# The second sum of four groups added by TensorE instead of VectorE in the last stage

## Time and profile before

| | us |
|---|---|
| median of 3 runs | 734.59 |
| profiled execution, own time | 735.17 |
| its span, first to last instruction | 733.4 |
| TensorE busy in the span | 626.0 (85%) |
| VectorE busy | 516.5 (70%) |
| ScalarE busy | 459.2 (63%) |
| POOL busy | 395.2 (54%) |

### The profile page before, as it was taken

How to read it: one execution, slowest core, us unless ns; L and a number is a source line. 1 busy time by engine, 2 the same in 40 slices (tenths; PEclk the granted TensorE clock), 3 DMA queues, 4 the chain that set the end, 5 groups by cost and what they waited for, 6 DMA issues and landing times.

```text
span 733.4 us, 13293 instructions
## 1 busy us (share of the span) xinstructions
PE 626.0 (85%) x3690; PEld 400.4 (55%) x3690; DVE 516.5 (70%) x1472; ACT 459.2 (63%) x929; POOL 395.2 (54%) x298
## 2 busy tenths in 40 slices
PE   6988979797999848799989999999999999984640
PEld 2454636373655546466656666666666666653420
DVE  3726596968878897877877777777777777650794
ACT  3788887647575643576656776766767767661044
POOL 0004212346777676667788776666666656576022
PEclk9999999679989956999999999999999999996555
DMA  7979999773232335456678977777776766755998
GB/s 243 419 308 150 219 266 300 184 198 118 88 120 89 118 118 154 130 103 115 118 133 174 186 154 117 109 116 115 109 115 103 116 111 104 107 65 59 317 226 145
DMA packets 110695, 114.34 MB, mean 156 GB/s; under 512 B 31426, under 2 KB 100306, under 8 KB 108962
## 3 DMA queue, kind: packets, MB, share of 16 engines
q0 software_dynamic: 34784, 49.70, 40.0%
q1 hardware_dynamic: 75842, 63.79, 29.0%
HBM read 54.94 MB, written 58.51 MB: 155 GB/s over the span
## 4 chain that ended last, share of the span: by engine, by line
PE 63%; DVE 22%; ACT 5%; issue 4%; DMA 4%; POOL 1%; DVEq 0%; SPq 0%; ACTq 0%; POOLq 0%
PE PS L544 9%; PE PS L695 8%; PE PS L697 8%; PE PS L696 8%; PE PS L723 4%; PE PS L709 4%; PE PS L724 4%; PE PS L725 4%; PE PS L684 4%; PE PS L579 3%; DMA sums<-arena 3%; DVE small L1161 2%; PE PS L571 2%; PE PS L601 2%; DVE W L1321 1%
## 5 line engine op out<-in xcount | busy, mean ns | idle before, releaser
L1078 POOL DMA_INDIRECT sums<-arena x143 | 222.6, 1556 | 103.7 <-DMA sums<-arena 55.2
L1046 POOL DMA_INDIRECT routed<-arena,small x104 | 119.3, 1148 | 71.5 <-DMA routed<-arena,small 58.7
L1468 DVE TENSOR_SCALAR arena<-PS,small 128x256 f32<-128x256 f32 x143 | 77.7, 544 | 83.1 <-ACT arena L979 82.9
L544 PE MATMUL PS<-arena 128*128 128x512 f32 x256 | 130.8, 648 | 4.1 <-ACT arena L784 2.2
L979 ACT ACTIVATE arena<-PS,small 128x256 f32<-128x256 f32 x143 | 67.8, 474 | 100.2 <-PE PS L697 100.2
L784 ACT ACTIVATE arena<-PS 128x512 f16<-128x512 f16 (+1 forms) x179 | 103.9, 590 | 32.6 <-PE PS L589 11.0
L695 PE MATMUL PS<-W,arena 128*128 x286 | 109.3, 382 | 0.0
L696 PE MATMUL PS<-W,arena 128*128 x286 | 109.2, 382 | 0.0
L697 PE MATMUL PS<-W,arena 128*128 x286 | 108.9, 381 | 0.0
L723 PE MATMUL PS<-W,arena 128*128 x286 | 78.6, 275 | 6.9 <-DVE arena L1442 5.7
L724 PE MATMUL PS<-W,arena 128*128 x286 | 78.7, 275 | 0.0
(11 more groups left out here) (183 smaller groups left out, 1019.0 us busy)
## 6 DMA issues: line engine op xcount, KB each, us to landing
arena<-routed SPq DMA_DIRECT2D x143, 128.0 KB, 2.5
W<-w_gu SPq DMA_DIRECT2D x8, 1024.0 KB, 23.9
W<-neg_mem POOLq DMA_DIRECT2D x16, 512.0 KB, 9.5
sums<-zero SPq DMA_DIRECT2D x2, 4096.0 KB, 35.6
W<-sums SPq DMA_DIRECT2D x16, 512.0 KB, 8.8
X<-x SPq DMA_DIRECT2D x8, 512.0 KB, 6.2
W<-w_dn SPq DMA_DIRECT2D x4, 1024.0 KB, 11.4
out<-X SPq DMA_DIRECT2D x7, 512.0 KB, 3.2
```

Source lines behind the costliest of these rows:

```text
L544: last = mm(PS[:, 2 + c % 2, :], WcT[:, k, c * P:(c + 1) * P], xT[:, k, :], start=(k == 0), stop=(k == KT - 1))
L1046: pool.indirect_dma_start(routed, bass.IndirectOffsetOnAxis(ap=idx, axis=0), rows[b][:, jk // TOPK, :], None).then_inc(rows_sent[lane], 16)
L1078: pool.indirect_dma_start(sums[j % SUMS], bass.IndirectOffsetOnAxis(ap=dst[j % MU], axis=0), yb[u], None, compute_op=ALU.add).then_inc(y_s ...
L1468: L.send(v.tensor_scalar(up[j % 2], acc[:, FF:2 * FF], gu_hi, gu_lo, ALU.min, ALU.max))
```

## The change

For groups 1, 3, 5 and 7 the second sum no longer goes through VectorE. `biases(g)` leaves the bias open in PSUM and adds to it, for each sub-row u, the product of `identY` (the identity times `y_inv`) and `z2[g]`, an f32 product of 128 rows and 256 columns; before the first such product TensorE waits for the load of `z2[g]`. `total(g)` then has one operation for these groups. `identY` is made by VectorE in the second stage, at tile 64. TensorE now waits until all eight groups' weights are copied, computes group 0's bias, multiplies constants 150 times into bank 7, and goes on with the biases of groups 1 to 7.

```diff
--- before.py
+++ after.py
@@ -59,6 +59,8 @@
 MAGIC = float(0x5F1FFFF9)
 ROOT_A, ROOT_B = 0.375 * 0.703952253, 0.375 * 0.703952253 * 2.38924456
 SUMS = 2
+HOLD = 150
+BY_PE = (1, 3, 5, 7)
 BATCHES = ((0, 1, 2, 3), (4, 5, 6), (7,))
 PART = 1024
 PARTS_GU, PARTS_DN = E * KT * 2 * FF // PART, E * KT * DIM // PART
@@ -322,6 +324,7 @@
         z2_in = [sem(f"z2_in{n}") for n in range(NBLK)]
         zero_ready, zero_sent, x1_sent = sem("zero_ready"), sem("zero_sent"), sem("x1_sent")
         sT_mm, sT_ready = sem("sT_mm"), sem("sT_ready")
+        identY_ready = sem("identY_ready")
         bias_mm, t_ready, rz_ready, yz_ready = sem("bias_mm"), sem("t_ready"), sem("rz_ready"), sem("yz_ready")
         out_sent = sem("out_sent")
         shift_ready, last_ready, last_sent = sem("shift_ready"), sem("last_ready"), sem("last_sent")
@@ -767,14 +770,23 @@
                     pe.wait_ge(t_ready, g - 2)
                 for u in range(BT):
                     last = mm(PS[:, 2 * (g % 3) + u // 2, (u % 2) * DIM:(u % 2 + 1) * DIM],
-                              sT[g][:, u * P:(u + 1) * P], Bdn[:, :], start=True, stop=True)
+                              sT[g][:, u * P:(u + 1) * P], Bdn[:, :], start=True, stop=g not in BY_PE)
+                    if g in BY_PE:
+                        if u == 0:
+                            pe.wait_ge(z2_in[g], 16)
+                        last = mm(PS[:, 2 * (g % 3) + u // 2, (u % 2) * DIM:(u % 2 + 1) * DIM],
+                                  identY, z2[g][:, u, :], start=False, stop=True)
                 last.then_inc(bias_mm, 1)
 
             pe.wait_ge(y2_ready, TILES + 2)
             pe.wait_ge(s_bdn, 16)
             for g in range(NBLK):
                 transpose_weights(g)
-            for g in range(NBLK):
+            pe.wait_ge(sT_ready, NBLK)
+            pe.wait_ge(identY_ready, 1)
+            biases(0)
+            keep_busy(HOLD, 7)
+            for g in range(1, NBLK):
                 biases(g)
 
 
@@ -1475,6 +1487,8 @@
                     table_cols(1)
                 if j == COUNT_AT + 3:
                     table_ints(1)
+                if j == EARLY:
+                    v.tensor_scalar(identY, ident, y_inv, None, ALU.mult).then_inc(identY_ready, 1)
 
             tiles(tile_step)
 
@@ -1484,6 +1498,9 @@
                 bias = PS[:, 2 * (g % 3):2 * (g % 3) + 2, :].rearrange("p b x -> p (b x)")
                 dve.wait_ge(blk_in[g], 32)
                 dve.wait_ge(bias_mm, g + 1)
+                if g in BY_PE:
+                    v.scalar_tensor_tensor(flat, flat, y_inv, bias, ALU.mult, ALU.add).then_inc(t_ready, 1)
+                    return
                 L(v.scalar_tensor_tensor(flat, flat, y_inv, bias, ALU.mult, ALU.add))
                 dve.wait_ge(z2_in[g], 16)
                 v.scalar_tensor_tensor(flat, flat2, y_inv, flat, ALU.mult, ALU.add).then_inc(t_ready, 1)
```

## The result

The changed kernel takes 751.37 us (median of four runs, 745.58 to 754.91) against 734.49 for the kernel before (four runs): a ratio of 1.026, 95% interval 1.020 to 1.032 (the quotient of the two medians is 1.023). Forecast were 742.9 us, 738.0 to 744.5. The direction was right, and so was the path (TensorE sets the pace, at half clock); the price of the work on that path was not.

The account below looks back on a forecast made before the run. VectorE was taken to bound the last stage; after the change half-clock TensorE sets the pace, moving the end from 732.5 to 740.8 (8.3 us). Profiled 735.17 + 8.3 = 743.5, so median 742.9 us, range 738.0 to 744.5.

Parts of the forecast that it names:

- What bounds the kernel, and what goes: VectorE bounds the last stage; dropping four second adds saves 5.1 us at most; an early final group alone gains little.
- The wait for the second sum: TensorE can begin group 1's second-sum products only at the landing, 687.7 us; biases of groups 2 to 7 queue behind.
- The constants: 150 products on idle TensorE before group 1's bias take 16.5 us, end before the second sum lands, cost nothing.
- The fall of the clock ahead of them: Possible half clock in the thin stretch before the constants, moving their end from 681.4 to 685.6 us.
- The clock: TensorE at half clock when group 1's second sum lands or soon after, and staying there through alternating and 16-row work.
- Rival B: TensorE at half clock for group 1, full from group 2 on; 738.5 us, chance 0.12.
- The sum at half clock: TensorE's last-stage products at 0.425 us each, 6.8 us per odd group, 3.4 per even; end 8.3 us later.
- exposed weight loads at a change of weights: Extra TensorE time when weights change, taken at nothing, at most 1 us over the groups.
- What a measurement can tell: Timing this kernel was said to tell a difference of 0.2%, 1.5 us, from no change.

Follow-up runs that it names:

- e7: Against the change: only group 7's second sum on TensorE, no constants; 46.0 us from group 1's second-sum landing to the end (45.7 before), ratio 1.001.
- e1: The change without its 150 constant products; 61.1 us from group 1's second-sum landing to the end (60.9 in the change), ratio to before 1.019.
- e3: The change with VectorE adding all second sums again, new order and constants kept; landing to end 46.8 us (45.7 before), ratio 1.007.
- e4: The change with bias products padded from 16 to 128 rows; landing to end 48.7 us (45.7 before), ratio to before 1.006.
- e6: e4 without the 150 constants; landing to end 49.3 us (48.7 in e4), ratio to before 1.005.
- e2: The change with odd groups' products reordered, 4 changes of form a group instead of 8; landing to end 56.7 us (60.9 in the change), median 745.41.
- e9: e4 with groups 4 to 7 on TensorE, 150 constants before group 3, 50 before group 4; landing to end 42.3 us (45.7 before), ratio 0.997.
- e10: e9 with groups 5 to 7 on TensorE, biases 3 and 4 after the 150 constants, then 60; landing to end 42.9 us, ratio to before 0.997.

## Why the prediction was wrong in size

- **What bounds the kernel, and what goes.** Right. VectorE bound the stage, and e7 shows that an early last group gains nothing that a profile can tell, since both chains at the end follow the second batch's statistics.
- **The wait for the second sum.** Right. Group 1's products began at the landing (682.92 against 682.88), and everything behind stood in TensorE's queue.
- **The constants.** Right for the change: 16.55 us forecast as 16.5, over 3 us before the landing, worth nothing (e1). That they cost nothing holds only because group 1 waits longer for something else; with VectorE adding the second sums they cost 1 us (e3), with the clock fallen ahead of them. The fall of the clock ahead of them, put as a possibility, came in e3 and not in the change.
- **The clock.** Right: 0.50 from the landing on, and neither the mixed nor the 16-row work raised it, though TensorE was busy without a gap. e4 and e6 show the other side: 128-row work raised it within 5 to 6 us. Rival B, by which the clock rises behind group 1, did not come. The Trainium skill (TensorE: Matmul & The Clock Gate, section "Why this matters for your kernels") has continuous work earn the full clock; the traces disagree for alternating and 16-row work (10.00 of 10.00 us busy at 0.50) and agree for 128 rows (e4, e6).
- **The sum at half clock: the step that failed.** It put each of an odd group's 16 instructions at 0.425 us, 6.8 a group, from a row where all had one form. They took 0.575 each, 9.2 a group. The term "exposed weight loads at a change of weights", which I bounded by 1 us over all groups from the 0.5 of one released group, was 0.30 us at every change, 8 x 0.30 = 2.4 in each odd group. I saw that the two forms alternate and weighed it for the clock only.
- **How that adds up**, counted from the landing: VectorE started group 1 at 8.3 us (forecast 6.5), group 3 at 20.9 (16.7), group 4 at 26.8 (22.7), group 6 at 37.2 (30.3), group 7 at 46.1 (37.3). The end moved by 15.2 instead of 8.3, so 6.9 are missing. Between the landing and group 6's start lie 7 + 8 + 8 = 23 changes of form (group 1's first one falls into its wait), and 23 x 0.30 = 6.9. The same count gives group 1 (6 changes, 1.8 late) and group 3 (14 changes, 4.2 late). In e2 there are 12 changes fewer up to group 6, 3.6 us, and two more instructions of group 1 run ahead of the landing, 0.85: 4.45 in all; its end came 4.2 earlier (60.9 - 56.7).
- The timed difference of the medians is 16.9 us; the 1.7 beyond the last stage are of the size by which the executions differ ahead of it, and no run traces them.
- **What a measurement can tell.** I put it at 0.2%. The intervals here are 0.3 to 0.9% wide on either side, so the gain of e9 and e10 could not be settled by time.

## What to carry to other kernels

Before work is moved to an engine that is idle, take its rate in the form in which it will run there: 16-row and 128-row products in turn ran at three quarters of the rate of either alone, and at half clock. With the bias products padded to the rows of the others (e4, e6), the alternation cost nothing and the clock came back within 6 us. That alone did not make the change pay: e4 still lost 3.0 us of the stage to the wait for group 1's second sum. Moving the work whose data come early (groups 4 to 7 in e9) shortened the stage by 3.4 us; the timed gain, a third of a per cent, is not shown.

## What the runs showed of the hardware that was not expected

- In f32 products of 256 columns, changing between operands of 16 and of 128 rows cost 0.30 us at half clock and 0.19 at full (pairs of 1.15 and 0.62 us instead of 0.85 and 0.43). Changing between two stationary operands of 128 rows cost nothing (e4, pairs of 0.85 at half clock), nor did adding to the place in PSUM that the product just before had written.
- With 16-row biases in every second pair, TensorE busy 7.90 of 7.90 us stayed at 0.50; with 128 rows in both, the granted clock rose from 0.50 to 1.00 5.0 us (e4) and 5.7 us (e6) after the work began.
